# A two-layer attention pipeline on one core: the steady loop written out, and VectorE's low halves of five kinds of products moved behind the first maximum of a step

## What is computed

```python
x = layernorm(x + attn(x, Wqkv, Wout))            # scores of 512 x 512 for each of 8 x 16 heads, softmax, times v
x = layernorm(x + xattn(x, ctx, w_q, ..., b_o))   # the same with keys and values of the context
x = layernorm(x + moe(x, ...))
```

## Time and profile before

| | us |
|---|---|
| median of three runs | 1383.52 (1378.53 to 1386.51) |
| the profiled execution's own time | 1384.98 |
| its span in the profile | 1383.2 |
| attention phase within it | about 1017.7 |
| granted TensorE clock, mean over the span | 0.979 |

### The profile page before, as it was taken

How to read it: one execution, slowest core, us unless ns; L and a number is a source line. 1 busy time by engine, 2 the same in 40 slices (tenths; PEclk the granted TensorE clock), 3 DMA queues, 4 the chain that set the end, 5 groups by cost and what they waited for, 6 DMA issues and landing times. The chain is left out here.

```text
span 1383.2 us, 27264 instructions
## 1 busy us (share of the span) xinstructions
PE 1306.8 (94%) x8312; PEld 774.9 (56%) x8312; DVE 1078.5 (78%) x2227; ACT 923.6 (67%) x1776; POOL 454.1 (33%) x487
## 2 busy tenths in 40 slices
PE   3999999999999999999999999999988999999996
PEld 2534444444444444444444444443466799999985
DVE  5889888888988987897888888889668755555557
ACT  3387777677777777777777777768736655565555
POOL 3334203401510240151024020102136636666663
PEclk9699999999999999999999999999999999999998
DMA  5453434344424433442443344234045466767695
GB/s 170 131 169 130 125 130 120 121 130 130 139 71 139 127 111 127 127 144 65 138 127 113 125 134 137 66 110 131 17 154 188 148 215 121 152 138 163 114 188 164
DMA packets 110089, 181.47 MB, mean 131 GB/s; under 512 B 20368, under 2 KB 67600, under 8 KB 105872
## 3 DMA queue, kind: packets, MB, share of 16 engines
q1 hardware_dynamic: 90576, 155.70, 35.6%
q0 software_dynamic: 18816, 23.60, 9.8%
q10 hardware_dynamic: 576, 0.79, 0.3%
HBM read 99.67 MB, written 79.30 MB: 129 GB/s over the span
## 5 line engine op out<-in xcount | busy, mean ns | idle before, releaser
L808 ACT ACTIVATE prob<-ps_sc 128x512 f32<-128x512 f32 x1024 | 551.1, 601 | 194.1 <-PE ps_sc L1070 193.4
L851 DVE TENSOR_REDUCE nm<-ps_ring 128x1 f32<-128x512 f32 x1024 | 638.5, 679 | 52.0 <-PE ps_ring L1055 51.5
L1055 PE MATMUL ps_ring<-qk 48*128 48x512 f32 x1024 | 407.4, 471 | 12.1 <-DMA qk<-hbm_self 7.4
L1070 PE MATMUL ps_sc<-qk 50*128 50x512 f32 x1024 | 388.5, 453 | 10.9 <-ACT prob L808 10.0
L1070 PEld LDWEIGHTS ps_sc<-qk 50*128 50x128 f32 x1024 | 161.2, 186 | 302.6 <-ACT prob L808 217.0
L1087 PE MATMUL ps_out<-prob,va 128*32 128x512 f32 x2048 | 276.9, 613 | 1.6 <-ACT ot L678 0.7
L1933 PE MATMUL ps_gu<-x2f,we 128*128 128x256 f32 (+1 forms) x1320 | 214.4, 317 | 1.0 <-ACT sg L1576 0.4
L1933 PEld LDWEIGHTS ps_gu<-x2f,we 128*128 128x128 f32 x1320 | 183.5, 191 | 15.0 <-ACT sg L1576 1.5
L1055 PEld LDWEIGHTS ps_ring<-qk 48*128 48x128 f32 x1024 | 166.8, 189 | 42.3 <-DVE nm L851 26.2
L607 POOL TENSOR_TENSOR rstd<-mv,eps 128x2 f32<-128x2 f32 x32 | 6.2, 195 | 345.3 <-DVE mv L939 345.3
L1933 PE MATMUL ps_dn<-we,hf 128*128 128x256 f32 x864 | 115.5, 285 | 2.9 <-DVE hf L1792 2.9
(11 more groups left out here) (185 smaller groups left out, 1595.2 us busy)
## 6 DMA issues: line engine op xcount, KB each, us to landing
qk<-hbm_cross SPq DMA_DIRECT2D x384, 64.0 KB, 2.3
qk<-hbm_self SPq DMA_DIRECT2D x372, 64.0 KB, 2.3
hbm_self<-stage SPq DMA_DIRECT2D x16, 1024.0 KB, 3.8
hbm_cross<-stage SPq DMA_DIRECT2D x16, 1024.0 KB, 4.1
slots_x<-zeros SPq DMA_DIRECT2D x8, 1360.0 KB, 5.9
xs<-slots_x SPq DMA_DIRECT2D x40, 272.0 KB, 4.0
weraw<-w_moe SPq DMA_DIRECT2D x11, 768.0 KB, 4.6
xin<-x SPq DMA_DIRECT2D x9, 512.0 KB, 4.3
```

Of the source, the lines that this page charges most:

```text
L808: nc.scalar.activation(prob[:, s % 2, j, :], ps_sc[:, score_bank(h.cur, HG * s + j), :], ACT.Exp, scale=HD ** -0.5).then_inc(exp_done[a], 1)
L851: nc.vector.tensor_reduce(nm[:, g % 2, r:r + 1], bank(slot), axis=AX.X, op=ALU.max, negate=True).then_inc(max_done[a], 1)
L1055: nc.tensor.matmul(bank(slot), qk[rows, 0, pair, P * c:P * c + P], qk[rows, 1, pair, :], start=True, stop=True).then_inc(smax_done[a], 1)
L1070: nc.tensor.matmul(ps_sc[:, score_bank(inst, n), :], qk[rows, 1, h // 2, P * c:P * c + P], qk[rows, 0, h // 2, :], start=True, stop=True). ...
```

## The change

The loop over k = 3 to 6 becomes a Python loop, so its body stands four times in the program with constants. On VectorE, tasks of the kinds in `AFTER_ACT` move behind the first maximum of their step, where the step has maxima; the other tasks stay ahead of it. TensorE, ScalarE and GpSimd keep their order.

```diff
+AFTER_ACT = ("ck", "cq", "xt", "nt0", "nt1")
...
-            with eng.Fori(3, B - 1) as k:
+            for k in range(3, B - 1):
                 half(first(k, second(k - 1)))
                 half(second(k, first(k)))
...
-                    for kind, n, b, of in h.behind(s):
-                        if kind not in ("nm0", "nm1"):
+                    behind = h.behind(s)
+                    for kind, n, b, of in behind:
+                        if kind not in ("nm0", "nm1") and not (turn and kind in AFTER_ACT):
                             task(kind, n, b, of.get((kind, n)))
                     for j in range(HG):
+                        if j == 1 and turn:
+                            for kind, n, b, of in behind:
+                                if kind in AFTER_ACT:
+                                    task(kind, n, b, of.get((kind, n)))
```

## The result

The changed kernel takes 1362.24 us (median of 4 runs, 1362.16 to 1363.34), the kernel before beside it 1383.42 (1378.53 to 1386.51): a ratio of 0.985, 95% interval 0.9831 to 0.9869. That is 21.2 us less; the forecast was 13.1 us less, 1370.3, and its range ended at 1363.5, 1.3 us above the measured time. So the direction was right, the time outside the range.

The account below looks back on a forecast made before the run. TensorE's order of work was taken to set the pace in the attention phase. The loop's 4.4 us and the order's 8.8 us made 13.2 us off, giving 1370.3 us against the median, range 1363.5 to 1378.0.

Parts of the forecast that it names:

- The loop: At the loop's three backward jumps in the attention phase: each costs 1.47 us, so writing the loop out saves 4.4 us.
- Rival C: At the borders of the loop body's copies: instruction loads stall an engine and give back 4.4 us, 1374.7 us; chance 0.08.
- Where the bank is wanted: Steps 0, 3, 4, 15 of cross-building halves: the later-freed bank just meets max3, 0 us; at worst 1.9 us lost.
- Step 1: Step 1 of eight halves: max2 waits 0.12 us for the low half, net gain 0.14 us each, 1.1 us in all.
- Steps 8 and 9 of `first`: In six halves: the nm transpose and w1 each go 0.27 us earlier, 0.54 us per half, 3.2 us in all.
- Step 13: Step with xt behind a layer norm, six halves: max0 fills VectorE's wait, 0.4 us each, 2.4 us in all.
- Steps 7 and 8 of `second`: In eight halves: VectorE's wait for nt0 is filled, TensorE gains 0.26 us each, 2.1 us in all.
- the order: VectorE's low halves moved behind the first maximum across the attention phase: gains by steps sum to 8.8 us.
- The clock: TensorE's five dips to half clock in the attention phase: the sum took no gain from them; fewer dips stood only as a rival.
- rival B: Attention phase: shorter waits leave out two or more of five clock dips, 3.4 to 8.5 us more, middle 1364.5; chance 0.17.
- Rival D: At 78 moved tasks: TensorE waits for the later-freed bank, 8.1 us slower at 0.16 us each, 1391.6 us; chance 0.05.
- A, hidden: Attention phase: removed waits only uncover others behind them, so the loop alone counts, 1379.1 us; chance 0.13.

Follow-up runs that it names:

- e1: The kernel before with only the loop written out, VectorE's old order kept: 1399.64 us, ratio 1.0014 to the kernel before (1400.12 us in that job).
- e8: The changed kernel with one more, unused maximum on VectorE ahead of xt's low half: 1372.54 us, ratio 0.9922 to the kernel before.
- e4: The changed kernel with xt left ahead of the maxima, only ck, cq, nt0 and nt1 moved: 1389.56 us, ratio 0.9924 to the kernel before.
- e10: The changed kernel with the hardware loop kept, so only the new order, measured again in another job: 1370.37 us, ratio 0.9893 to the kernel before.
- e9: The kernel before with only the loop written out, measured again in another job: 1378.42 us, ratio 0.9957 to the kernel before.

## Why the prediction was wrong, point by point

- **The loop, 4.4 us.** Right: 1.47, 1.41 and 1.52 us off the three steps in e1. The product that waits for the late exponential is the fourth score product of the step, not the third. The registers, taken at nothing, cost about 0.6 us: steps 9 and 10 of `second` are 0.08 and 0.05 shorter in straight code. Rival C did not come true: no engine stalls at a copy's border, and the copies took 58.4 us each (`first` of periods 3 to 5, `second` of 3 to 6). But I read too much into the straight halves when I said that none of their steps was lengthened: step 10 of `second` in period 2 is 4.57 us long before as after (4.23 in e8), where its likes in straight code have 4.23, and the copy of period 6 got a step longer by 0.3 in the same way. The Trainium skill, "Runtime: NRT & Kernel Launch", section "Instruction fetch mechanics", has it that streaming a long program costs little that shows. The traces agree: 0.3 us in one step is all that the copies added, and whether a load of instructions is its cause is not shown.
- **Where the bank is wanted, a tie.** Nearly right: steps 0 are longer by 0.05. But steps 3 and 4 gained up to 0.1 each: they hold two jobs, the second takes max1's bank, and that is read earlier. I had looked at max3 alone.
- **Step 1, 0.14 each.** Under: 0.25. Max2 did wait 0.11 for ck's low half (1.98 into the step instead of 1.87), but the score product beside it does not wait, max3 followed 0.23 behind, and the transpose of ot lost nothing; it gained the whole 0.26.
- **Steps 8 and 9 of `first`, 0.54 each.** Right: 0.55. Both holds on TensorE, nm's and w1's, went.
- **Step 13, 0.4 each.** Right: 0.59 off step 13, 0.15 given back in step 14, 0.45 in all in the six halves. `own2` and `cross5`, which I left out, gained 0.3 each in the same way.
- **Steps 7 and 8 of `second`, 0.26 each.** Over: 0.20.
- Together the order gave 11.7 us instead of 8.8. What the sum left out or took too low are steps 1, 3, 4 and 13, the last in two halves that it did not count.
- **The clock, the step that failed.** The sum kept all five dips, a term put at nothing. "If shorter waits leave two or more of the five out" stood as a rival with 0.17, because the same step had passed without a dip in passes two and three. All five went, 6.3 us, inside that rival's 3.4 to 8.5. I had taken the two passes without a dip as evidence that a step's place in time decides as much as its waits. The rows had more to say: the five dips lay at the eight places and nowhere else in the steady part, and the change shortens just those steps. I had also placed them "at the end of a step 12 or 13"; they begin about 1 us into the step that follows. In the six places with a step 13 of 4.0 us, 12 of 30 dipped, with the step shortened, none of 48. A part was luck: the profile of before had five dips, the four others with long steps 13 had two to four; and why the two dips of `own2` and `cross5` (1.7 us) went is open. The Trainium skill, "TensorE: Matmul & The Clock Gate", section "A second HAM failure mode: psum-queue depth-cycling", tells of another kernel where frequent small idle times between groups of matmuls came with a swinging clock. It pointed the right way; the runs agree for the six places by the length of the step, though not by the idle time recorded in it, 0.60 us before and 0.59 after.
- **The range.** The middle of rival B with the order at 8.8 is 1364.4, a microsecond above the range's lower end. With B come true and the order's error of 2.9 us on top, the two gains stack; I had treated them as alternatives, each within the range alone.
- **Rival D, slower, and A, hidden.** Neither: the one step where the bank is later than its user (step 1) still gained.

## What to carry to other kernels

An engine that waits at the head of its step for a partner can take the first piece of work that is ready instead; what it costs is a later release of the partner's buffer, and the check is when its next user comes. Price the TensorE clock with the order: note at which steps the granted clock falls, and if a change shortens the waits just ahead of such a fall, count the dips as going. Where it shortens only what comes behind the fall, these runs give no ground to count on it. A hardware loop's jump is cheap to find (a wait without a cause, once per pass, here on ScalarE), and what it costs hangs on the order of the work behind it: 4.4 us for three jumps here with one order on VectorE, 6.3 to 7.1 with the other.

## What the runs showed of the hardware beyond that

- The stretches at half clock at the eight places lasted 3.4 us each, two of the 18 twice that (one in e4, one in e8). One of 3.4 us made its step longer by 1.4 to 1.6 us in the six places, in `own2` and `cross5` by 0.7 to 0.8 where the step is 3.1 us long and by 1.3 in e10, where it is 2.6.
- Behind a backward jump ScalarE issued nothing for 2.2 to 2.4 us, and VectorE's first instruction stood up to 2.8 us after its last one; TensorE's own first products came on time each time.
- One job differed from the others by about as much as the change: in it the kernel before took 1400.1 us instead of 1383, and its profiles show ScalarE waiting up to 6.7 us at a time for loads in the experts' phase, while the attention phase was as long as elsewhere (straight loop alone 987.9 us there, 990.4 in e9).
